# A graph-network kernel: own rows of layer 0 added by TensorE, places found earlier, own bits counted by ScalarE, first rows loaded behind gathers

## The reference

```python
h = jnp.maximum(_layernorm(x, axis=-1), 0.0)
x = x + _L0_gnn_ref(h, adj, L0_gnn_W, L0_gnn_a, L0_gnn_gamma, L0_gnn_beta)
...
    # in _L0_gnn_ref
    Wh = jnp.einsum('bnf,fo->bno', h, W)
    ...
    scores = jnp.where(adj[None] > 0, e, NEG_INF)
    attention = jax.nn.softmax(scores, axis=2)
    h_prime = jnp.einsum('bij,bjo->bio', attention, Wh)
    mean = h_prime.mean(axis=(0, 2), keepdims=True)
    var = h_prime.var(axis=(0, 2), keepdims=True)
    h_prime = gamma[None, :, None] * (h_prime - mean) * jax.lax.rsqrt(var + BN_EPS) + beta[None, :, None]
    out = h_prime + h
    return jax.nn.elu(out)
```

## Time and profile before

| | |
|---|---|
| time, median of 3 runs | 1465.96 us (1465.49 to 1466.02) |
| time of the profiled execution | 1465.91 us |
| its span in the profile | 1464.2 us |
| VectorE busy | 1195.2 us, 82% |
| GpSimd busy | 960.1 us, 66% |
| TensorE busy | 956.3 us, 65% |
| ScalarE busy | 855.2 us, 58% |
| first gather of layer 0 / of layer 1 | 147.0 / 348.9 us |

### The profile page before, as it was taken

How to read it: one execution, slowest core, us unless ns; L and a number is a source line. 1 busy time by engine, 2 the same in 40 slices (tenths; PEclk the granted TensorE clock), 3 DMA queues, 4 the chain that set the end, 5 groups by cost and what they waited for, 6 DMA issues and landing times. The chain is left out here.

```text
span 1464.2 us, 16972 instructions
## 1 busy us (share of the span) xinstructions
PE 956.3 (65%) x4663; PEld 672.8 (46%) x4663; DVE 1195.2 (82%) x1552; ACT 855.2 (58%) x2899; POOL 960.1 (66%) x983
## 2 busy tenths in 40 slices
PE   3665447542898886498899966566616755756591
PEld 1433113212687775387788832222205655652240
DVE  5994689985999999999999159999976998947571
ACT  5864336664575465356787726777983548654330
POOL 4214776626887866398787468887666787647770
PEclk9887777866899998799999987877856777887796
DMA  9838987514222431012111054533226564438875
GB/s 286 272 102 299 323 243 239 167 58 141 60 83 84 117 92 37 29 35 75 51 51 37 30 166 134 146 115 110 84 97 189 156 185 115 132 119 248 240 236 139
DMA packets 108294, 202.19 MB, mean 138 GB/s; under 512 B 48320, under 2 KB 56800, under 8 KB 106144
## 3 DMA queue, kind: packets, MB, share of 16 engines
q0 software_dynamic: 38384, 128.36, 28.6%
q1 hardware_dynamic: 68840, 72.46, 15.6%
q10 hardware_dynamic: 968, 0.21, 0.1%
HBM read 149.97 MB, written 55.21 MB: 140 GB/s over the span
## 5 line engine op out<-in xcount | busy, mean ns | idle before, releaser
L1092 ACT ACTIVATE big<-big 128x64 f32<-128x64 f32 x1496 | 370.8, 339 | 172.1 <-DVE big L1869 161.0
L806 POOL TENSOR_TENSOR big<-big 128x512 f32<-128x512 f32 x373 | 376.5, 1040 | 123.0 <-DVE big L1869 108.1
L1912 DVE TENSOR_REDUCE big<-big 128x32 f32<-128x2048 f32 (+4 forms) x126 | 297.7, 2362 | 4.3
L1447 PE MATMUL PS<-big,ident 128*128 128x512 f32 x348 | 188.8, 704 | 117.2 <-ACT big L1092 70.5
L1466 PE MATMUL PS<-ident,big 128*128 128x128 f32 x1740 | 232.5, 294 | 42.2 <-POOL big L806 35.1
L1466 PEld LDWEIGHTS PS<-ident,big 128*128 128x128 f32 x1740 | 218.4, 154 | 52.1 <-issue 24.8
L1904 DVE TENSOR_TENSOR big<-big,PS 128x2048 f32<-128x2048 f32 (+4 forms) x84 | 198.5, 2363 | 17.3 <-PE PS L1478 14.5
L1447 PEld LDWEIGHTS PS<-big,ident 128*128 128x128 f32 x348 | 76.3, 226 | 228.0 <-issue 203.8
L779 POOL DMA_INDIRECT big<-tab,SI x142 | 138.0, 972 | 48.6 <-issue 45.0
L779 POOL DMA_INDIRECT big<-h_rows,SI x142 | 137.9, 971 | 38.4 <-issue 29.3
L1463 PE MATMUL PS<-big,ident 128*128 128x512 f32 x174 | 105.9, 769 | 55.3 <-POOL big L806 51.8
(11 more groups left out here) (182 smaller groups left out, 1682.3 us busy)
## 6 DMA issues: line engine op xcount, KB each, us to landing
big<-in_adj SPq DMA_DIRECT2D x16, 1024.0 KB, 6.4
own<-big SPq DMA_DIRECT2D x48, 256.0 KB, 2.0
big<-own SPq DMA_DIRECT2D x48, 256.0 KB, 3.4
big<-xs SPq DMA_DIRECT2D x8, 1024.0 KB, 8.7
tab<-big SPq DMA_DIRECT2D x32, 132.0 KB, 2.8
own<-big SPq DMA_DIRECT2D x32, 132.0 KB, 1.9
big<-own SPq DMA_DIRECT2D x16, 264.0 KB, 4.0
big<-in_x SPq DMA_DIRECT2D x16, 256.0 KB, 6.8
```

What stands on the lines that cost most here:

```text
L806: ins = pool.tensor_tensor(bd(wbuf[:, i % NWB, j, :]), bd(rows[:, k + j, :]), over_d(S[:, h, k + j, :], B), ALU.mult)
L1092: ins = act.activation(to, row, ACT.Copy, scale=S[:, h, k + j, b:b + 1])
L1447: mm = pe.matmul(to.rearrange("p (b d) -> p b d", b=B), ident[:, :], rows[:, k, :].rearrange("p (b c) -> p b c", b=B)[:, :, 0:D], start=(k ...
L1912: run(dve.tensor_reduce(scores(u, t)[:, h, k:k + n, :].rearrange("p k b -> p (k b)"), bd(prod[:, 0:n * E]), AX.X, ALU.add))
```

## The change

Four edits. In layer 0 the addition of the own rows goes from VectorE to TensorE, as two identity matmuls into one of the banks 4 to 6, behind the slots of a later tile; VectorE's minimum and its maximum read that bank. `find_places` moves from the middle of round 14 to the end of round 13, and rows 12 and 13 change their rounds. The sum of the own bits goes to ScalarE, as one activation with a sum over all 2048 bits of a node, behind row step 17. And `load_rows(0)` waits for tile 1's gathers.

```diff
-ROWS_ENDED = {..., 13: [9], 14: [10, 11],
-              15: [12, 13, 14, 15]}
+ROWS_ENDED = {..., 13: [9], 14: [10, 11, 12],
+              15: [13, 14, 15]}
...
                 for i in range(4):
-                    if i > 0:
-                        g = 4 * i - 3
-                        sp.wait_ge(gathered[g % NRB], gathered_by(g))
+                    g = max(4 * i - 3, 1)
+                    sp.wait_ge(gathered[g % NRB], gathered_by(g))
                     load_rows(i)
...
                 rows_step(s)
+                if s == NT + 1:
+                    act.wait_ge(own_cleared, NT)
+                    act.activation(masks[0], own_bits.rearrange("p t j -> p (t j)"), ACT.Sign, accum_out=small[:, 5, 0:1])\
+                       .then_inc(own_counted, 1)
...
                         add_up(0, t)
+                    t = m - 4
+                    if 0 <= t < NT:
+                        if t % 4 == 0:
+                            pe.wait_ge(x_part_loaded[t // 4], 32)
+                        if t >= 3:
+                            pe.wait_ge(x_added, t - 2)
+                        pe.matmul(bank(4 + t % 3), ident[:, :], H0[:, t, :], start=True, stop=False)
+                        pe.wait_ge(attended, t + 1)
+                        pe.matmul(bank(4 + t % 3), ident[:, :], no[:, t % 4, :], start=False, stop=True).then_inc(own_added, 1)
...
-                if c == RANKED_AFTER + 1:
-                    find_places()
                 for t in ROWS_ENDED.get(c, []):
                     end_row(t)
+                if c == RANKED_AFTER:
+                    find_places()
             find_caps()
-            dve.wait_ge(own_cleared, NT)
-            run(dve.tensor_reduce(diag, own_bits, AX.X, ALU.add))
             run(dve.tensor_reduce(nvalid, valid[:, :, :], AX.X, ALU.add))
             run(dve.tensor_tensor(bad, deg, cap, ALU.is_gt))
-            run(dve.tensor_scalar(tmp, diag, 1.0, None, ALU.is_lt))
-            run(dve.tensor_tensor(bad, bad, tmp, ALU.add))
             run(dve.scalar_tensor_tensor(tmp, nvalid, 1.0, deg, ALU.add, ALU.not_equal))
             run(dve.tensor_tensor(bad, bad, tmp, ALU.add))
-            tell(dve.tensor_reduce(allbad, bad, AX.X, ALU.add), bad_made, 1)
+            run(dve.tensor_reduce(allbad, bad, AX.X, ALU.add))
+            dve.wait_ge(own_counted, 1)
+            run(dve.tensor_scalar(tmp[:, 0:1], diag[:, 0:1], float(NT), None, ALU.is_lt))
+            tell(dve.tensor_tensor(allbad, allbad, tmp[:, 0:1], ALU.add), bad_made, 1)
...
                 def elu_low(t):
-                        o = no[:, t % 4, :]
-                        dve.wait_ge(attended, t + 1)
-                        dve.wait_ge(x_part_loaded[t // 4], 32)
-                        run(dve.tensor_tensor(o, H0[:, t, :], o, ALU.add))
-                        tell(dve.tensor_scalar(na[:, t % 2, :], o, 0.0, None, ALU.min), elu_in, t + 1)
+                        dve.wait_ge(own_added, t + 1)
+                        tell(dve.tensor_scalar(na[:, t % 2, :], bank(4 + t % 3), 0.0, None, ALU.min), elu_in, t + 1)
                 def elu_add(t):
-                        o = no[:, t % 4, :]
-                        run(dve.scalar_tensor_tensor(X[:, t, :], o, 0.0, X[:, t, :], ALU.max, ALU.add))
+                        if t % 4 == 0:
+                            dve.wait_ge(x_part_loaded[t // 4], 32)
+                        run(dve.scalar_tensor_tensor(X[:, t, :], bank(4 + t % 3), 0.0, X[:, t, :], ALU.max, ALU.add))
```

More of the change, by code:

```diff
@@ L148 @@
 RANK_STEP = 11
-ROWS_ENDED = {4: [0], 5: [1], 6: [2], 7: [3], 8: [4], 9: [5], 10: [6], 11: [7], 12: [8], 13: [9], 14: [10, 11],
-              15: [12, 13, 14, 15]}
+ROWS_ENDED = {4: [0], 5: [1], 6: [2], 7: [3], 8: [4], 9: [5], 10: [6], 11: [7], 12: [8], 13: [9], 14: [10, 11, 12],
+              15: [13, 14, 15]}
 STEPS_WITH = {3: [0], 4: [1], 5: [2], 6: [3], 7: [4], 8: [5], 9: [6], 10: [7], 11: [8], 12: [9], 13: [10], 15: [11]}
@@ L309, in program @@
         own_cleared = sem("own_cleared")
+        own_counted = sem("own_counted")
         mask_used = sem("mask_used")
@@ L386, in program @@
         x1_added = sem("x1_added")
+        own_added = sem("own_added")
         mean_made = sem("mean_made")
```

## The result

The changed kernel takes 1510.26 us (median of 4 runs, 1509.01 to 1511.85), beside 1465.72 us for the kernel before on the same chip: 1.0306 times as long, 95% interval 1.0288 to 1.0324, so 44.5 us more. The profiled execution took 1510.96 us with a span of 1509.2 us, 45.0 us more than before's 1464.2 us. In the following, ratios compare runs on the same chip, because the kernel before itself gave medians of 1460.6 to 1465.7 us. A ratio and the quotient of the two medians beside it can differ by up to 0.2%. A few disturbed runs are left out.

What follows compares the result with a forecast made beforehand. VectorE's instruction stream was taken to bound layer 0's attention, transfers the prologue's end. New VectorE waits less savings summed to +40.4 us, the other edits at 0: 1465.91 + 40.4 = 1506.3 us, own range 1492 to 1520, 80% range 1482 to 1520.

Steps and rivals of the forecast that it cites:

- The mechanism: Layer 0: `elu_low` waits for the whole slot sum plus 2.0 us after the weighing; tile 12 stands 3.3 us.
- the prediction's running sum: Layer 0, tile by tile: VectorE's new waits less its savings, added up to 40.4 us.
- The term that was too small: TensorE's slot sums in layer 0, taken from the earlier trace: 4.53 us at tile 4, 14.9 us at tile 8.
- (a): Rival: TensorE, being busier, stays at 2.4 GHz in layer 0; 1482 us, chance 0.08.
- Parts 1 to 3 at 0: Earlier places, own-bit check on ScalarE, loads behind tile 1's gathers: taken as 0, with -3 to +5 us around.
- The minimum from a bank: `elu_low`'s minimum in layer 0 takes 0.69 us reading a bank, where from SBUF it takes 0.43 us.
- (b): Rival at `elu_low`: TensorE's slack covers the own addition, VectorE keeps 13 later savings, 7.9 us; 1458 us, chance 0.06.
- (c): Rival, above 1522 us: clock rises later in each burst, or loads and late row add their bounds, 1525; chance 0.05.
- (d): Rival: no effect, since other waits of layer 0's stage take up the new ones; chance 0.01.

Runs made afterwards that it cites:

- Turning the order: The changed kernel with TensorE's own addition ahead of the tile's slot sum in the same round: 1456.44 us, ratio 0.9950.
- parts 1 to 3: The changed kernel with layer 0's own rows added by VectorE as before, the other three edits kept: 1461.01 us, ratio 1.0012.
- part 3 alone: The kernel before with only the first rows' loads put behind tile 1's gathers: 1464.26 us, ratio 1.0008.
- one more matmul: The changed kernel with H0's matmul issued twice, the second recomputing the same bank: 1510.75 us, ratio 1.0339.
- part 4 first: The kernel before with own rows added on TensorE ahead of the slot sum, and the 128x8 product reading a bank: 1450.43 us, ratio 0.9919.
- the PSUM run: The kernel before with only the 128x8 product reading one factor from a PSUM bank: 1455.79 us, ratio 0.9964.

## Why the prediction was right

**The mechanism** held as put: the path from the end of the weighing to the minimum is the whole sum and 2.0 us (8.63 = 6.70 + 1.93 us at tile 12), VectorE stands for what exceeds its other work of 4.91 us (4.95 us in the prediction), and the loop moves everything behind it. Turning the order took the waits away. At tile 8, where the sum started 0.49 us after the weighing, the path was 15.30 us for a sum of 12.99 us. Forecast +40.4 us, measured +44.5 us, within its own range. A small part of that nearness is luck: the sums were short by more than the total shows, and layer 3, of which the prediction said nothing, gave 2.6 us back.

**By tile.** How much the end of the weighing moved against before, tile by tile, beside the prediction's running sum:

| up to the weighing of tile | 8 | 9 | 10 | 11 | 12 | 13 | 14 | 15 | layer 1's first gather |
|---|---|---|---|---|---|---|---|---|---|
| predicted, us | 10.5 | 21.8 | 27.1 | 29.9 | 34.0 | 36.6 | 39.2 | 41.1 | 40.4 |
| measured, us | 12.9 | 21.5 | 28.4 | 32.9 | 37.4 | 40.4 | 43.5 | 46.3 | 47.3 |

**The term that was too small** is the length of the sums. The prediction used for tiles 4 to 15 durations that add up to 88.6 us; they took 95.9 us, 7.3 us more, close to the 6.9 us of the last column. Tiles 4, 10 and 12 were taken at 4.53, 6.25 and 6.23 us, as in the earlier trace rows, and took 7.37, 8.59 and 6.70 us. Those rows were of bursts that followed pauses of 2.7 to 3.2 us, and the same argument of the prediction that spoke against rival (a), that pauses become 5 us and longer, should have made them dearer in the sum. At the rows after long pauses, 7.59 us for 5 slots, 7.73 for 6 and 8.74 for 7, the eight tiles with 5 to 7 slots make 63.3 us; they were taken at 54.4 us and took 61.6 us. The length of the pause alone doesn't give the duration, though: tiles 4 and 12 took 7.37 and 6.70 us after 5.10 and 5.11 us, and tile 4's sum took 4.54 us after a pause of 3.67 us in the run with parts 1 to 3 and 7.49 us after 2.99 us with part 3 alone. What else sets it no run shows. Tile 8 went the other way, 12.99 us for a predicted 14.9 us, so its wait was 10.23 us and not some 12 us.

**Parts 1 to 3 at 0** was right within what can be measured. Places at 109.60 (109.5), the wait 3.12 us (3.0); row 10's end came at 114.56 (114.4), and the first gather came 1.2 us sooner, inside the 2.0 us allowed. Not foreseen was VectorE's wait of 4.47 us for row 12, and the last row's end came at 129.82, 4.4 us later than before; its scatter at 137.87 still fed a first gather at 145.84. Tile 0 came to VectorE 4.9 us after its first gather where it took 7.3 us before, 2.4 us sooner (up to 2 us in the prediction). The check on ScalarE took 1.89 us and a read of 0.19 us, hidden.

**The minimum from a bank.** 0.691 us, sixteen times, where from SBUF it is 0.429 us. Here the trace agrees with the Trainium skill (VectorE: DVE Perf Modes, "Why PSUM operands drop a tier"), which has a float32 operand in PSUM processed at one element per cycle, and the 0.69 us that the prediction took was right.

**The rivals.** (a), the upper clock throughout, didn't come: the clock of 250 to 300 us fell to 0.81. Denser bursts did bring a little of it in the run with one more matmul: 2.5 us or more over its last four sums, beyond what executions of the same code differ by. The rule that the prediction cites for (a) from the Trainium skill (TensorE: Matmul & The Clock Gate, Part 1), that sustained activity releases the throttle, agrees with these rows; with pauses of 5 us and more it didn't carry the kernel to the upper clock. (b), 1458 us, is what the slack pays once the order is turned: layer 1 then starts 7.3 us sooner than before, where (b) had said 7.9 us, and the medians are 4.2 us apart (0.9950 by the ratio). (c) and (d) didn't come.

## What to carry to other kernels

Work that is moved to an engine with slack must be put into that engine's order where its inputs are old, ahead of whatever the receiver itself has just released; the same 32 matmuls cost 45 us behind the sum and brought some 4 to 7 us ahead of it. When a loop of two engines loses its overlap, price the second engine's bursts by those rows of the trace that follow pauses as long as the new ones, and keep a range of some us, because the same burst after the same pause took 6.05 to 7.57 us here (tile 4, after 5.10 us). And compare executions at a marker close behind the edit (here layer 1's first gather): the end of the kernel carries variations of several us from stages that were not touched.

## What the hardware showed unexpectedly

A stage that the edits don't touch took either some 251 us or 245 us: layer 1's second attention, between its first gather and that of layer 2. The changed kernel's execution had 251.2 us, that with one more matmul 245.4 us. VectorE's timeline of the changed kernel, and GpSimd's at the same time, show where:

```profile
1042.54 7.56 DVE L2027 TENSOR_TENSOR nshift<-ln 128x8 f32<-128x8 f32 x1 [0.29 <-ACT ln L1178]
1050.13 3.35 DVE L1921 TENSOR_TENSOR big<-big,PS 128x3072 f32<-128x3072 f32 x1
```

```profile
1042.81 5.03 POOL L807 TENSOR_TENSOR big<-big 128x512 f32<-128x512 f32 x5
1047.82 1.26 POOL L816 TENSOR_TENSOR big<-big,rows 128x512 f32<-128x512 f32 x1
1049.04 1.03 POOL L791 TENSOR_TENSOR big<-big,stats 128x512 f32<-128x512 f32 x1
```

A product of 128x8 elements, both operands in SBUF, usually takes 0.17 us. Here it took 7.56 us and ended at 1050.10, when GpSimd's seven elementwise instructions in a row (1042.81 to 1050.07) were done. The kernel before has the same at its 994.97, 7.62 us. With one more matmul the product came 0.54 us ahead of GpSimd's series, where above it is 0.27 us, and wasn't caught:

```profile
1049.05 0.17 DVE L2028 TENSOR_TENSOR nshift<-ln 128x8 f32<-128x8 f32 x1
```

```profile
1049.59 5.03 POOL L807 TENSOR_TENSOR big<-big 128x512 f32<-128x512 f32 x5
```

Of the nine profiled executions that read both operands from SBUF, seven have an instance of 7.47 to 7.71 us and take 250.6 to 251.3 us for the stage; the two without (parts 1 to 3, one more matmul; 1.4 us at most) take 245.0 and 245.4 us. The Trainium skill (SBUF — State Buffer, "SBUF: two separate sides") says that a VectorE operation with two SBUF inputs and a GpSimd one that reads SBUF exclude each other on a shared port pair, and that the one that starts first has it for its whole instruction. By the records the product started 0.27 us before GpSimd's series and still ended with it, so VectorE got no turn between seven instructions; the page's sentence alone doesn't give that. With one operand in a bank of PSUM the same product is never long (min/median/max 161/163/164 ns), and the three profiled executions with that edit take 241.0 to 243.7 us for the stage:

```profile
L2031 DVE TENSOR_TENSOR nshift<-ln,PS x16: 161/163/164, 873.3 to 1069.5; 128x8 f32<-128x8 f32 x16
```

In the profiled execution of the kernel before with this edit the stage is 7.6 us shorter (243.7 against 251.3 us), but layer 0 ended 1.9 us later than in that of the kernel before. That, and executions of the kernel before that lack the long instance, fit the 5 us of the whole time; how often it is lacking no run counts.

The same stage has a second stall of this kind, in the addition of the mask to 56 scores (two SBUF operands again). Here it is in the kernel before with the edit:

```profile
927.41 6.69 DVE L1848 TENSOR_TENSOR big<-big,SI 128x56 f32<-128x56 f32 x1
```

It isn't the first stall moved: it comes some 60 us ahead of the product's place, and executions have it without the edit (the changed kernel, 6.64 us at 973.63) and lack it with the edit (part 4 first, 0.22 us). Nor does it show in the length of the stage, which is 251.2 us with it in the changed kernel and 251.3 us without it in the kernel before.

The same fits the own additions that part 4 takes from VectorE: they took 0.92 us instead of 0.69 us in the eight late rounds, and each of these eight began some 0.7 us after the start of a centring of 1.03 us on GpSimd (tile 8's own addition at 276.31, the centring at 275.64). That the port is the cause was argued from these overlaps and from the PSUM run; no run isolated it.
